# A graph kernel's start with x in five pieces, all statistics ahead of the norms, and units on ScalarE

## What is computed

```python
def _layernorm(x, axis=-1, eps=1e-05):
    m = jnp.mean(x, axis=axis, keepdims=True)
    v = jnp.var(x, axis=axis, keepdims=True)
    return (x - m) / jnp.sqrt(v + eps)
...
    norm2 = jnp.linalg.norm(x, axis=1, keepdims=True)
    cos = beta[0] * (x @ x.T) / (norm2 @ norm2.T + 1e-07)
    masked = cos + (1.0 - adj) * -1000000000.0
    P = jax.nn.softmax(masked, axis=1)
    return P @ x
...
    deg = jnp.clip(jnp.sum(adj, axis=1, keepdims=True), 1.0)
    h_neigh = adj @ h / deg
    return h @ W_self + h_neigh @ W_neigh
...
    h = jnp.maximum(_layernorm(x, axis=-1), 0.0)
    x = x + _L0_gnn_ref(h, adj, L0_gnn_beta)
    h = jnp.maximum(_layernorm(x, axis=-1), 0.0)
    x = x + _L1_gnn_ref(h, adj, L1_gnn_W_self, L1_gnn_W_neigh)
```

## Time and profile before

| what | us |
|---|---|
| median of 3 runs | 504.84 |
| lowest, highest | 504.59, 505.44 |
| the profiled execution | 502.87 |
| its span, first to last instruction | 500.9 |

### The profile page before, as it was taken

The page is one execution under the profiler, slowest core; times in us unless marked ns, Lnnn a source line. Parts: engine busy times, 40 slices in busy tenths (PEclk is TensorE's granted clock), DMA queues, the critical chain, the costliest instruction groups (busy, mean ns, idle before and its releaser), DMA issues.

```text
span 500.9 us, 12746 instructions
## 1 busy us (share of the span) xinstructions
PE 471.2 (94%) x5392; PEld 397.7 (79%) x5392; DVE 279.8 (56%) x686; ACT 298.1 (60%) x427; POOL 297.0 (59%) x261
## 2 busy tenths in 40 slices
PE   0768999999999999999999999999799999999996
PEld 0636788888788888888888888877688888888895
DVE  6975666567566585656765856757632321322153
ACT  2979787866986759876798598688730201110121
POOL 3889887877897768986799688888750000000000
PEclk9989999999999999999999999999999999999999
DMA  8057865655776557754676476563010000000001
GB/s 248 12 183 282 273 204 175 224 178 183 252 249 221 181 161 249 245 217 157 225 244 236 167 227 223 205 196 107 3 34 1 22 22 22 1 22 22 22 1 43
DMA packets 31549, 74.39 MB, mean 149 GB/s; under 512 B 2560, under 2 KB 15104, under 8 KB 31488
## 3 DMA queue, kind: packets, MB, share of 16 engines
q1 hardware_dynamic: 31488, 73.54, 43.8%
HBM read 71.43 MB, written 2.10 MB: 147 GB/s over the span
## 4 chain that ended last, share of the span: by engine, by line
PE 87%; DVE 5%; POOL 3%; DMA 2%; ACT 2%; issue 1%; SPq 0%; POOLq 0%; DVEq 0%; ACTq 0%
PE ps L1078 23%; PE ps L941 17%; PE ps L952 9%; PE ps L1005 6%; PE ps L1002 6%; PE ps L1004 6%; PE ps L979 5%; PE ps L982 5%; PE ps L981 5%; PE ps L1063 2%; PE ps L1052 2%; DVE adj_t L665 1%; DVE adj_t L644 1%; DMA stage<-in_adj_dram 1%; DMA x_sb<-in_x_dram 1%
## 5 line engine op out<-in xcount | busy, mean ns | idle before, releaser
L407 POOL TENSOR_TENSOR near<-word,adj_t 128x1024 f32<-128x1024 f32 x72 | 145.2, 2016 | 57.4 <-DVE word L778 56.4
L561 ACT ACTIVATE word<-ps,small 128x512 f16<-128x512 f32 x144 | 135.6, 942 | 70.8 <-PE ps L941 67.0
L778 DVE TENSOR_TENSOR word<-ps,word 128x512 f16<-128x512 f32 x144 | 106.3, 739 | 105.4 <-ACT ps L562 105.3
L1078 PE MATMUL ps<-table,adj_t 128*128 128x257 f16 x1024 | 116.8, 274 | 0.0
L941 PE MATMUL ps<-unit_t 128*128 128x512 f16 x432 | 106.7, 381 | 4.7 <-DVE word L778 4.7
L1078 PEld LDWEIGHTS ps<-table,adj_t 128*128 128x128 fp8e4 x1024 | 99.3, 98 | 13.0
L562 ACT ACTIVATE ps<-ps,small 128x512 f32<-128x512 f32 x144 | 107.2, 744 | 0.0
L1002 PE MATMUL ps<-table,near 128*128 128x129 f16 x576 | 102.6, 219 | 4.0 <-POOL near L407 2.6
L1005 PE MATMUL ps<-table,near 128*128 128x129 f16 x576 | 102.8, 222 | 0.0
L1004 PE MATMUL ps<-table,near 128*128 128x128 f16 x576 | 102.6, 219 | 0.0
L979 PE MATMUL ps<-table,far 128*128 128x129 f16 x448 | 79.9, 219 | 0.3
(11 more groups left out here) (94 smaller groups left out, 490.6 us busy)
## 6 DMA issues: line engine op xcount, KB each, us to landing
stage<-in_adj_dram SPq DMA_DIRECT2D x128, 512.0 KB, 4.4
x_sb<-in_x_dram SPq DMA_DIRECT2D x4, 512.0 KB, 6.2
x_again<-in_x_dram SPq DMA_DIRECT2D x8, 256.0 KB, 5.6
out_dram<-x_sb SPq DMA_DIRECT2D x7, 256.0 KB, 2.3
out_dram<-x_sb SPq DMA_DIRECT2D x1, 192.0 KB, 2.0
stage<-in_L_gnn_W_neigh_dram SPq DMA_DIRECT2D x1, 64.0 KB, 2.6
stage<-in_L_gnn_W_self_dram SPq DMA_DIRECT2D x1, 64.0 KB, 2.5
out_dram<-x_sb SPq DMA_DIRECT2D x1, 64.0 KB, 1.7
```

The lines of the kernel that those rows point to most:

```text
L407: pool.tensor_tensor(ring(near, k), ring(word, k), adj_t[:, near_adj(k)], ALU.mult).then_inc(s_near, 1)
L561: act.activation(half(word16, k, c, 0, HIGH, TPS), score(k, c), ACT.Exp, bias=exp_bias, scale=exp_scale)
L778: dve.tensor_tensor(half(word16, k, c, 0, LOW, TPS), score(k, c), half(word16, k, c, 0, HIGH, TPS), ALU.subtract).then_inc(s_elo, 1)
L1078: return pe.matmul(ps[:, agg_bank(g) + t, 0:TW], adj_t[:, at:at + P], tab(b), start=(b == 0), stop=(b == T - 1))
```

## The change

x comes in five pieces, of 4, 4, 8, 8 and 8 tiles. VectorE computes all statistics before the first norm, no longer adds epsilon, multiplies or clamps; GpSimd has a small step with these factors ahead of each power. GpSimd computes no units any more; ScalarE computes those of group 0 in between rows of h, and those of groups 4 to 7 behind the exponentials of pairs 2, 4, 6 and 8. VectorE keeps groups 1, 2 and 3, with 3 inside the low parts of pair 0. The inverse norms of the last two pieces stand behind the masks of pairs 0 and 2. The table's first group is made before the flag. TensorE's order of sums, transposes and first scores differs, transposes 0 to 2 have PSUM banks of their own (3, 4, 2), and SyncE requests the first two far tiles right behind the first two near ones. The lead of the conversions is 3 as before. The form of attention for small norms is changed along with it; these inputs do not take it.

```diff
@@ RING, PIECE
-    RING = [("unit", 0), ("unit", 1), ("score", 0, 0), ("score", 0, 1), ("score", 1, 0), ("score", 1, 1), ("unit", 2)]
+    RING = [("score", 0, 0), ("score", 0, 1), ("score", 1, 0), ("score", 1, 1)]
...
-    XP = 4
-    TX = T // XP
+    PIECE = [slice(0, 4), slice(4, 8), *(slice(t, t + 8) for t in range(8, T, 8))]
+    XP = len(PIECE)
+    GROUPS = [p.stop // TPS for p in PIECE]
...
-            return 5 + AT["unit", g] % 3
+            return (3, 4, 2)[g] if g < 3 else 5 + AT["unit", g] % 3
@@ sync
+            load_near(0)
+            load_near(1)
+            load_far(FAR[0])
+            load_far(FAR[1])
+            for k in range(2, NP):
+                sp.wait_ge(s_adjd, k - 1)
+                load_near(k)
...
@@ gpsimd
-                pool.tensor_tensor(rstd[:, part], var_e[:, part], neg_half, ALU.pow).then_inc(s_rstd, 1)
+                pool.tensor_scalar(var_e[:, part], mv_v[:, part, 1], HS ** -2, EPS * HS ** -2, ALU.mult, ALU.add
+                                   ).then_inc(s_scaled_e, 1)
+                pool.wait_ge(s_scaled_e, i + 1)
+                pool.tensor_tensor(scale_h[:, part], var_e[:, part], neg_half[:, 0:part.stop - part.start], ALU.pow
+                                   ).then_inc(s_rstd, 1)
...
             inverse_std(2)
+            inverse_std(3)
+            inverse_std(4)
             inverse_norm(0)
-            units(0)
-            inverse_std(3)
             inverse_norm(1)
-            scaled_inverse_norm(1)
             convert(0)
             inverse_norm(2)
+            convert(1)
             pool.wait_ge(s_least, 1)
...
-            inverse_norm(3)
-            units(7)
-            convert(1)
+            low_parts(0)
             convert(2)
             convert_far(2)
...
                 mask_near(k)
-                if s == 0 and k % 2 == 0:
-                    low_parts(k // 2)
+                if k in (0, 2):
+                    inverse_norm(3 + k // 2)
+                if s == 0 and k % 2 == 1 and (k + 1) // 2 < NS:
+                    low_parts((k + 1) // 2)
@@ scalar
+            first_h(0, 0, 4)
+            first_h(1, 4, 8)
+            first_h(2, 8, 16)
+            first_h(3, 16, 22)
+            units(0)
+            first_h(3, 22, 24)
+            first_h(4, 24, 27)
+            unit_high(0)
+            first_h(4, 27, T)
+            act.wait_ge(s_h, TPS)
+            table_high(0)
             act.wait_ge(s_flag, 1)
...
-                    if k == 1:
-                        unit_high(2)
+                    if k <= 1:
+                        unit_high(k + 1)
...
+                    if k in (2, 4, 6, 8):
+                        units(k // 2 + 3)
@@ vector
             variances(2)
             scales(1)
+            variances(3)
+            scales(2)
+            variances(4)
+            scales(3)
             norms(0)
-            scales(2)
-            variances(3)
             norms(1)
-            scales(3)
+            scales(4)
             norms(2)
-            units(1)
             unit_low(0)
             norms(3)
+            norms(4)
+            dve.wait_ge(s_norm2, XP)
...
-            unit_low(1)
-            units(2)
+            units(1)
             dve.wait_ge(s_flag, 1)
...
-            units(4)
-            units(5)
-            units(6)
+            units(2)
...
                     low_part(k, 0)
+                    if k == 0:
+                        units(3)
                     low_part(k, 1)
-                unit_low(2)
+                    unit_low(1 + k)
@@ tensor
-            sum_of_h(0, TX)
+            sum_of_h(0, 16)
             unit_transpose(0)
-            sum_of_h(TX, T - TX)
+            scores(0)
+            for i in range(3):
+                score_product(1, 0, i)
+            sum_of_h(16, T)
             unit_transpose(1)
-            scores(0)
-            sum_of_h(T - TX, T)
-            scores(1)
-            unit_transpose(2)
+            for i in range(3):
+                score_product(1, 1, i)
             pe.wait_ge(s_first, 5)
             pe.wait_ge(s_mean, 1)
             for k in range(NP):
                 if k + 2 < NP:
                     scores(k + 2)
+                    if k == 0:
+                        unit_transpose(2)
```

More of the change, by code:

```diff
@@ L98, in u_rows, with piece_of @@
             return half[:, (a - lo) * D:(b - lo) * D]
+        mv_v = mv.rearrange("p (t c) -> p t c", c=2)
+        def piece_of(g):
+            return min(i for i in range(XP) if GROUPS[i] > g)
         def by_tile(ap):
@@ L660, in norms @@
             def norms(i):
-                part = slice(i * TX, (i + 1) * TX)
-                for t in range(i * TX, (i + 1) * TX):
+                for t in range(PIECE[i].start, PIECE[i].stop):
                     dve.wait_ge(s_h, t + 1)
@@ L667, in norms @@
                         scale=1.0, scalar=0.0, op0=ALU.mult, op1=ALU.add, accum_out=norm2[:, t:t + 1])
[L668 to L669 removed]
+                last.then_inc(s_norm2, 1)
             def units(g):
[L673 removed]
+                dve.wait_ge(s_rnorm, piece_of(g) + 1)
                 for t in range(g * TPS, (g + 1) * TPS):
[L675 to L676 removed]
+                    dve.tensor_scalar(u_rows(t, t + 1), h_rows(t, t + 1), rnorm[:, t:t + 1], None, ALU.mult).then_inc(s_unit, 1)
             def unit_low(g):
@@ L763, in scale_scores @@
                 p, f = PAIR[k][1], ring(word, k, c, 1)
+                for i in range(XP):
+                    if PAIR[k][0] == 0 and 2 * p + c == PIECE[i].start:
+                        dve.wait_ge(s_rnorm, i + 1)
+                        dve.tensor_scalar(inv_eps[:, PIECE[i]], rnorm[:, PIECE[i]], EPS_COS, None, ALU.mult).then_inc(s_inv_eps, 1)
+                        dve.wait_ge(s_inv_eps, i + 1)
                 at = 3 * (2 * k + c)
```

114 lines of the change are left out of this document (49 added, 65 removed).

## The result

The changed kernel has a median of 506.33 us (505.64 to 507.84, ten runs), the kernel before 504.6 us beside it (502.82 to 505.44, ten runs): 1.0043 times the time, 95% interval 1.0027 to 1.0059. The change makes the kernel slower, by about half a per cent. The median lies 0.2 us from the 506.1 forecast, but the profiled executions are further apart: 505.79 us after (span 504.0) and 502.87 before (span 500.9), 2.9 us and not 1.3. Both facts have to be explained.

What follows compares the result with a forecast made beforehand. The prediction took the start of pair 2's near products, after which TensorE has no gaps, as the bound. Terms +0.2 + 1.1 - 0.4 + 0.4 = +1.3 on 504.84 gave 506.1 us, range 504.2 to 507.9.

Steps and rivals of the forecast that it cites:

- the sum is read as a difference: Last step: the summed terms, +1.3, were added to the earlier kernel's median of 504.84, giving 506.1 us.
- near 2: Start of pair 2's near products, from which TensorE runs without gaps: 48.79 us before, forecast to come later.
- A: Length from the start to the flag, ahead of the first exponential: +0.2 us, bounds -0.7 to +0.6.
- the clock: TensorE's low granted clock after early idle stretches, no longer covered by ScalarE's DMA wait: +0.4 us.
- Rival 4: GpSimd binds after all, its queue full from mask 0 to mask 5: 507 us, chance 0.02.
- Rivals 1 and 2: First: units unblocked, no low clock, 505.1, chance 0.25. Second: norms unblocked, unit_high(2) hardly waits, 503.8, chance 0.15.
- The relay: After the last variance at 14.9: GpSimd's scaling and power, ScalarE's units and high part, VectorE's low part, norms from 22.7.
- B: ScalarE's queue from the first exponential to pair 3's: +1.1 us (0.3 to 1.5), including 0.75 waiting and 0.6 for blocked units.
- The four known edits: In ScalarE's queue: table_high(0) and the DMA wait out, unit_high(1) and units(4) in, together -0.22 us.
- C: What TensorE takes over of ScalarE's delay, part of it vanishing behind mask_far(2): -0.4 us.
- rival 3: Low clock falls on scores, turns and attention of pairs 1 to 2, not hidden: further 1.4, 507.5 us, chance 0.18.
- Near products 0: Start of pair 0's near products on TensorE: forecast at 35.9 to 36.8 us, against 37.84 before.

Runs made afterwards that it cites:

- the first experiment: Changed kernel with GpSimd's conversion of tile 1 moved from ahead of the flag to behind low_parts(0): 504.92 us, 1.0025 times the kernel before.
- last experiment: Changed kernel with 36 late, 28 early and 30 further extra TensorE products in idle stretches, results unused: 504.49 us.
- the one with two edits: Changed kernel with conversion 1 behind the flag, transposes of group 2 behind those of group 1, and 36 extra late products: 503.08 us, 0.9983 of before.

## Why the prediction was right in its number, and where it was wrong

The median was 1.5 to 1.7 us above before, the sum said +1.3. That match is partly luck. The step "the sum is read as a difference" to the median took 504.84, which lies in the upper group of before, while the median after lies in its lower group. Like with like the change costs 3.1 (506.0 less 502.93). By the prediction's own terms, measured in the profiled execution as moves of near 2 (3.26 in all), two fell short: A by 1.15 and the clock by 0.8.

**Where the end is set: right.** The marker at near products 2 held in every kernel: span less marker is 451.9 to 452.4 us in the eleven profiled executions whose clock stayed at 1.00 near 364, and 453.5 to 453.6 in the three where it fell. GpSimd wasn't on the path: it doesn't wait itself between masks 0 and 4, but up to near 2 neither ScalarE nor TensorE has a wait that ends with a mask. Rival 4's mechanism shows only when the transposes are moved. Rivals 1 and 2, without a block and without a low clock, fall with the norm of 1.16 and the units of 2.83.

**A, forecast +0.2, measured +1.35**, outside its bounds of -0.7 to +0.6. The block of one norm was right, 0.88 for 0.85. The relay ahead of it was about 1.0 too short. In the first experiment, without any block, the first exponential still came 0.42 behind that of the kernel before, where the forecast without a block was -0.7. The last variance stands at 15.55 for 14.9: beta landed at 3.91 instead of 3.64, so statistics began at 5.30, not 5.00, and the 32 rows with their waits and scale steps took 10.25 and not 9.9. GpSimd's last power of that chain took 1.78 and the next 1.18 (1.64 and 1.03 in the earlier trace rows), so ScalarE's units began at 19.35 for 18.3, and norms resumed at 23.67 for 22.7. Each stage of the relay was given its best duration. The other 0.15 lie between VectorE's last step on the smallest norm and the first exponential, 1.87 (28.28 to 30.15) for 1.72.

**B, forecast +1.1, measured +2.30** (45.12 less 41.47 is 3.65, less A). The four known edits, -0.22 in sum with the missing DMA wait among them, were right. The wait of unit_high(2) was 2.65 where 0.75 and 0.6 for the block were taken. At full clock it is 1.49 (last experiment), so queue and block together were priced well, 1.35 for 1.49. The other 1.16 are the low clock, which the sum has as a term of its own. (-0.22 and 2.65 make 2.43; the missing 0.1 are shorter steps.)

The block itself also went as foreseen. The four units were allowed to last from 29.1 to 32.0 and took 2.83; that they were one long wait and three short steps wasn't foreseen, and changes nothing in the sum. What it costs shows at the low part of pair 1, chunk 0 (line 808; the row holds two):

```profile
33.50 0.95 ACT L594 ACTIVATE word<-ps,small 128x512 f16<-128x512 f32 x1
...
35.79 1.47 DVE L808 TENSOR_TENSOR word<-ps,word 128x512 f16<-128x512 f32 x2
```

It starts 2.29 us behind the exponentials of that pair, where the prediction had 1.53: 0.76 late for a forecast of 0.6. In the first experiment it was 1.88 (35.01 less 33.13), 0.35 late, and the wait 1.08, so lateness and wait move together.

**C, forecast -0.4, measured -0.39** (marker +3.26 against +3.65). Right, mechanism included: exponentials (3,1) now end at 48.11 and their low part starts at 48.46, 0.35 later, where it was 0.71 before.

**Clock, forecast +0.4, measured 1.16** at the wait of unit_high(2) and 1.5 of the time. The mechanism was named, its size and place were not: the term weighed low part (0,0), which didn't wait for it, and it lay on the scores of pair 2 and the transposes of group 2. That is among the places where rival 3 had it ("on scores, turns and attention of pairs 1 to 2"). Its 507.5 lay 1.4 above the forecast, and the upper group of after, which is to be set against the 504.84 of before, lies at 507.6 to 507.8. So the rival given 0.18 was nearer to the kernel than the forecast was.

Added up: 1.35 + 1.14 - 0.39 + 1.16 = 3.26, with the clock taken out of B. The forecast's +1.3 became 506.1, near the median, since it was added to a number of the upper group.

**Near products 0, forecast at 35.9 to 36.8, came at 38.90**, later than the 37.84 of the earlier trace rows. Mask 0 was done at 37.40, but on TensorE six score products at low clock and the transposes stood in front of them. This was the one sign where the forecast pointed the wrong way.

The Trainium skill (SBUF — State Buffer, "Who interferes with whom") says that whoever issues first gets the ports shared by VectorE and GpSimd for the whole instruction, and that the other "fully blocks". The norm of 1.16 us beside a conversion of 1.05 and a unit of 2061 ns beside a mask of 2.01 agree with it. The unit of 2248 ns doesn't quite: it began ahead of both conversions and ended behind both. Two things aren't slowed where the rule would have them wait: the twelve units of the earlier trace rows beside GpSimd's short 128x128 steps, and the norm at 23.67 (0.28 us), which reads SBUF twice, beside a power of GpSimd. So the rule doesn't give a price without the trace.

## What to carry to other kernels

An idle wait is the cheapest place for work: units put into VectorE's and ScalarE's wait for a flag cost nothing, while the same units beside long GpSimd instructions cost three to six times their own time, and a wait on the one side only hands the block to the next group. Price a group of short VectorE steps beside long GpSimd ones by how long GpSimd goes on without a pause, and not by one of its instructions. When TensorE has an idle stretch ahead of work that something waits for, price that work at half clock too. Take the stages of a chain of small steps with their waits as the trace has them, not with their best durations. Before comparing medians of kernels that differ by less than 1%, look at whether their times lie in groups, and compare group with group.

## What the runs showed of the hardware

- Four 128x128 f32 scalings on VectorE take 0.85 us. They took 2.83 us beside two conversions of 1.04, where one lasted 2.25 across both conversions and the rest 0.28 each; 2.46 in the kernel where GpSimd waited; and 4.94 beside a mask of 2.01, low_parts and conversions, where each waited anew (the shortest 0.87, the longest 2.06 us). The low parts (line 808, which read PSUM and SBUF and write f16) and the norms beside a power of GpSimd (the norm at 23.67, 0.28, beside the power from 22.32 to 23.98) weren't slowed.
- A 2.6 us idle stretch of TensorE near 362 us is followed in some executions by more than 3 us at 0.50 clock (363.9 to 367.3 in the one shown) and in others by none; span less marker differs by 1.5 us between them (453.5 and 452.0). 36 small products in it, about 2.1 us of work, left a spread of 0.2 to 0.7 us in four kernels and of 1.7 in the fifth, the one with two edits.
- In the execution of the first experiment the clock row reads 1.00 for 12 to 38 us, although its nine score products took 4.02 us as at half clock. In the kernel before it reads 1.00 around 19 us, although its four transposes at 18.95 took 1.11. Durations of like products are the surer sign.
